# The third tile's modulation product in split operands, in a four-stage gated kernel on one core

## The chip, the cores and the metric

One NeuronCore of a Trainium2 chip runs the whole program. The metric is the device time of one execution in microseconds (us), as the median of several runs. TensorE is PE in the profile, VectorE is DVE, ScalarE is ACT, GpSimd is POOL and SyncE is SP; SPq and ACTq are DMA issues from these engines.

## The reference, cut to what matters

Four residual stages work on x of 4 sequences x 1024 tokens x 512 channels: an MLP with a selected expert, a selected linear layer, a recurrent gated block, and another selected linear layer. The change is in the third, of which these lines matter (`x` is the stage's input):

```python
ctx = causal_ema(x, tau_ctx)
wg = sigmoid(concat([x, ctx]) @ Wg.T + bg);  gated = x * wg
h1 = gelu(x @ Wn1.T + bn1)                     # 128 channels per token
mod = 0.5 + sigmoid(h1 @ Wn2.T + bn2)          # 4 channels per token
traces = [causal_ema(gated * mod[d], tau_raws[d]) for d in range(4)]
temporal = sum_d traces[d] * blend_w[d]
gate = sigmoid(temporal @ Wtemp.T + btemp)
soma = gelu(x @ Wsoma.T + bsoma)
out = layernorm((soma * gate) @ Wout.T) * gamma + beta;  x = x + out
```

## The kernel before, in words

Channels lie on the 128 partitions and tokens along the free axis; a tile is 512 tokens of one sequence, so there are eight tiles, 0 to 7. Matrix products with 128x128 weights are made from split operands: `split_product` issues three matmuls, high weight by high input (L1434), high weight by low input (L1435), low weight by high input (L1436). The high part is a copy by ACT into the type fp32r, the low part is what DVE leaves after subtracting it (`low_part`, L1869).

The order of work on each engine is written out by hand. The engines run their own lists and meet at semaphores. The first two residual stages fill about the first 700 us. Then the recurrent block and the last layer are pipelined by tile: round r of the loops (`for r in range(1, NT)` on PE, `for r in range(2, NT)` on ACT and DVE) takes the gate sums of tile r, the temporal and output products of tile r-1, and the last layer of tile r-2.

The modulation layer of tile i goes as follows. `n1(i)` on PE sums x @ Wn1 into a PSUM bank (L1579 is its last matmul). `h1_of(i)` on ACT makes h1 by GELU (L1058). `mo(i)` on PE multiplies by the 4 columns of Wn2. For tiles 0 to 2 this is one ordinary float32 `matmul` (L1592, two records each in the trace), placed for tile 2 after the first chunk of `gate(2, 0)`, that is after 6 of its 24 matmuls. For tiles 3 to 7 it is a `split_product`, after the second chunk (12 matmuls), and it needs `h1_hi_of(i)` on ACT (L1064) and `h1_low(i)` on DVE (L1869, h_lo). `mod_of(i)` on ACT (L1068) takes the hyperbolic tangent, ACT adds 2 (L1074), writes the four rows to DRAM (L1077) and reads them back on all partitions into mod_t (L1083). The first use of mod_t for a tile is the DVE line `drive` (L2095).

The other chain in the place of the change belongs to tile 1, chunk 3. On DVE `traces_a` to `traces_d` make, from gated, four drives (L2095), four scans (L2108) and three additions (L2123) into temporal. `temporal_hi(1, 3)` on ACT rounds it (L1104), `temporal_low(1, 0)` and `temporal_low(1, 2)` on DVE make the low parts of chunks 0-1 and 2-3 (L1869, temporal_lo). `te(1, 0)` on PE, the first product after `gate(2, 0)`, waits for the first of these low parts, and the next three `te` follow it.

The low part of Wn2 (`wn2_hl`, shown as wn_hl in the trace) is made once, ahead of `temporal_low(1, 0)`.

Of the kernel before, what the change touches and what calls it, by code (L numbers as in the profile page):

```python
# [15 lines left out]
TAUS = 4  # L16
# [25 lines left out]
def build(nc, x, tok16, tok8, small, fc1_w, fc2_w, exp_w, exp_b, l1_w, l1_b, wg, wn1, wsoma, wtemp, wout,  # L42
# [15 lines left out]
    with ctx:  # L58
# [3 lines left out]
        def place(name, kib, shape, dt=F32):  # L62
            return nc.alloc_sbuf_tensor_at(name, [P] + shape, dt, offset=base + int(kib * KIB))
# [7 lines left out]
        def sem(name):  # L71
            return ctx.enter_context(nc.semaphore(name))
# [73 lines left out]
        wn2_hl = place("wn2_hl", 127, [2, P], F32R)  # L146
# [97 lines left out]
        s_wn2 = sem("s_wn2")  # L244
# [201 lines left out]
        def n1_bank(i):  # L446
            return bank[5 if i > 1 else 7]
# [37 lines left out]


        def mo_split_no(i):
            return max(0, i - 2)

        def ss_split_no(i):  # L490
            return min(i, LAST - 1 - 1)
# [10 lines left out]
        def rows_stored(i):  # L502
            return (s_mst, 16 * i) if i else (s_mst_first, 16)
# [416 lines left out]
        def _(eng):  # L920
            on = Once(eng)
# [130 lines left out]
            def h1_of(i):  # L1052
                on.wait_ge(s_pe["N1"], i + 1)
                if i:
                    on.wait_ge(*rows_stored(i - 1))
                if i > 2:
                    on.wait_ge(s_out[1], 16 * HALVES * (i - 2))
                eng.activation(h1[:, :], n1_bank(i)[:, :], ACT.Gelu, bias=bn1_sb[:, 0:1]).then_inc(s_h1, 1)  # L1058


            def h1_hi_of(i):
                on.wait_ge(s_h1, i + 1)
                on.wait_ge(s_pe["SS"], i - 1)
                eng.activation(h1_hi[:, :], h1[:, :], ACT.Copy).then_inc(s_h1hi, 1)  # L1064

            def mod_of(i):
                on.wait_ge(s_pe["MO"], i + 1)
                eng.activation(mod_row[0:TAUS, :], mo_bank(i)[0:TAUS, :], ACT.Tanh, bias=bn2_sb[0:TAUS, 0:1],  # L1068
                               scale=0.5).then_inc(s_mod, 1)


            def modulation_out(i):
                on.wait_ge(s_mod, i + 1)
                eng.activation(mod_row[0:TAUS, :], mod_row[0:TAUS, :], ACT.Identity, bias=two_sb[0:TAUS, 0:1]  # L1074
                               ).then_inc(s_mod2, 1)
                on.wait_ge(s_mod2, i + 1)
                eng.dma_start(mod_dram[i], mod_row[0:TAUS, :]).then_inc(s_mst, 16)  # L1077
# [18 lines left out]
            def temporal_hi(i, m):  # L1096
                on.wait_ge(s_add, SH * (KC * i + m + 1))
                if i:
                    on.wait_ge(s_pe["OU"], KC * i)
                    if m == KC - 1:  # L1100
                        on.wait_ge(s_pe["SS"], min(i, LAST - 1))
                else:
                    on.wait_ge(s_fc2, UNITS)
                eng.activation(ts_hi[:, m, :], temporal[:, m, :], ACT.Copy).then_inc(s_temphi, 1)  # L1104

            def te_tanh(i, m):
                on.wait_ge(s_pe["TE"], KC * i + m + 1)
                ps = te_bank(m)
                eng.activation(ps[:, :], ps[:, :], ACT.Tanh, bias=btemp_sb[:, m:m + 1], scale=0.5
                               ).then_inc(s_gate, 1)  # L1110
# [244 lines left out]
            soma_of(1, 3)  # L1355

            for r in range(2, NT):
                if r == 2:
                    h1_of(r)
                    temporal_hi(r - 1, 3)  # L1360
                else:
                    temporal_hi(r - 1, 3)
                    h1_of(r)
                    h1_hi_of(r)
                mod_of(r)
                modulation_out(r)
                modulation_back(r)
                wg_tanh(r, 0)
                te_tanh(r - 1, 0)
                for m in range(KC):  # L1370
                    x3_hi_of(r - 2, m)
                for m in range(1, KC):
                    te_tanh(r - 1, m)
                for m in range(KC):
                    spikes_hi(r - 1, m)
                wg_tanh(r, 1)
                y_of(r - 2, 0)
                y_of(r - 2, 1)
                if r < LAST:
                    y_of(r - 2, 2)  # L1380
                    y_of(r - 2, 3)
                wg_tanh(r, 2)
                o_of(r - 1, 0)
                o_of(r - 1, 1)
                wg_tanh(r, 3)
                o_of(r - 1, 2)
                o_of(r - 1, 3)
                if r <= LAST - 1:
                    sumsq_hi(r - 1)
                soma_of(r, 0)  # L1390
                soma_of(r, 1)
                for m in range(SH):
                    temporal_hi(r, m)
                if r < LAST:
                    rows_std(r - 1)
                soma_of(r, 2)
                soma_of(r, 3)
# [31 lines left out]
        def _(eng):  # L1429
            on = Once(eng)  # L1430
# [149 lines left out]
                mm.then_inc(s_pe["N1"], 1)  # L1580

            def mo(i):
                if i > 2:

                    on.wait_ge(s_wn2, 3)
                    on.wait_ge(s_h1hi, mo_split_no(i))
                    on.wait_ge(s_h1lo, mo_split_no(i))
                    split_product(mo_bank(i)[:, :], wn2_hl[:, 0, :], wn2_hl[:, 1, :], h1_hi[:, :], h1_lo[:, :],
                                  True, True).then_inc(s_pe["MO"], 1)
                    return  # L1590
                on.wait_ge(s_h1, i + 1)
                eng.matmul(mo_bank(i)[0:TAUS, :], wn2_sb, h1[:, :], start=True, stop=True  # L1592
                           ).then_inc(s_pe["MO"], 1)
# [3 lines left out]
            def gate(i, m):  # L1597
                if m == 0:
                    if i > 1:
                        on.wait_ge(s_soma, KC * (i - 1) + 1)  # L1600
                    elif i:
                        on.wait_ge(s_soma, 1)
                    else:
                        on.wait_ge(s_mod, 1)
                elif m == 1:
                    if i > 1:
                        on.wait_ge(s_mod, i + 1)
                    elif i:
                        on.wait_ge(s_soma, 2)
                    else:  # L1610
                        on.wait_ge(s_x1, KC * LAST)
                elif m == 2:
                    if i >= 2:
                        on.wait_ge(s_z, KC * (i - 1))
                    else:
                        on.wait_ge(s_gated, KC if i else 1)
                else:
                    if i >= 2:
                        on.wait_ge(s_y, KC * (i - 2) + (3 if i < LAST else 1))
                    else:  # L1620
                        on.wait_ge(s_gated, 3 if i else 2)
                        if i:
                            on.wait_ge(s_mod, 2)
                on.wait_ge(s_wg[m], 16)
                for c in range(KC):
                    x2 = slot(i, c)
                    for k, before in ((2 * c, 0), (2 * c + 1, 1)):
                        at = LEAD - before
                        mm = split_product(wg_bank(i, m)[:, :], wg_hl[m][:, k, 0, :], wg_hl[m][:, k, 1, :],
                                           x2[:, 0, at:at + TOK],  # L1630
                                           x2[:, 1, at:at + TOK], c == 0 and not before,
                                           c == KC - 1 and before == 1)
                    if m == 0 and c == (1 if i > 2 else 0) and i > 1:
                        mo(i)
                mm.then_inc(s_pe["WG"], 1)

# [228 lines left out]
        def _(eng):  # L1865
            on = Once(eng)

            def low_part(lo, raw, hi):
                return eng.tensor_tensor(lo, raw, hi.bitcast(F32), ALU.subtract)  # L1869
# [261 lines left out]
            def traces_b(i, c):  # L2131
                trace_of(i, c, 0)
                trace_of(i, c, 1)
                drive_of(i, c, 2)
                add_of(i, c, 1)

            def traces_c(i, c):
                trace_of(i, c, 2)
                drive_of(i, c, 3)
                add_of(i, c, 2)  # L2140
# [10 lines left out]
            def h1_low(i):  # L2151
                on.wait_ge(s_h1hi, mo_split_no(i))
                low_part(h1_lo[:, :], h1[:, :], h1_hi[:, :]).then_inc(s_h1lo, 1)
# [260 lines left out]
            traces_d(1, 2)  # L2414
            traces_a(1, 3)
            traces_b(1, 3)
            traces_c(1, 3)
            traces_d(1, 3)
            on.wait_ge(s_wn2, 2)
            low_part(wn2_hl[:, 1, 0:TAUS], wn2_sb, wn2_hl[:, 0, 0:TAUS]).then_inc(s_wn2, 1)  # L2420
            temporal_low(1, 0)
            temporal_low(1, 2)
            for r in range(2, NT):
# [135 lines left out]
```

## Time and profile before

| | |
|---|---|
| median of 3 runs | 1328.03 us (1327.83 to 1331.12) |
| the profiled execution's own time | 1327.52 us |
| its span, first to last instruction | 1325.8 us |
| PE busy | 1309.0 us (99%) |
| DVE busy | 1060.6 us (80%) |
| ACT busy | 667.6 us (50%) |
| mean granted TensorE clock | 1.000 |

The span leaves 1.72 us of the profiled execution's time around it. A busy share is an average over stages. A matmul's record is 0.39 us long, but matmuls overlap in the pipeline, and one starts every 0.23 us when nothing holds them; so distances between starts are the durations to count with on PE. DVE records overlap in the same way by some 0.07 us.

### The profile page before, as it was taken

Reading aid. Unit: us, or ns where it says so; the run is one execution under the profiler, and the core shown is the slowest. Engines: PE = TensorE matmul, PEld = TensorE weight load, DVE = VectorE, ACT = ScalarE, POOL = GpSimd, SP = SyncE. Lnnn points to the kernel's source line nnn. Section 1 sums busy time; section 2 is a strip of 40 time slices with the busy share of each in tenths; the row PEclk is TensorE's granted clock in tenths of the full one; section 3 lists DMA queues with packets and bytes.
Section 4 is the critical chain, followed back from the end, with each engine's and each line's share of the span. In section 5 each row is a group of like instructions: output and inputs, shape, how many; then the busy total and the mean of one; then the engine's idle time right before and its main releaser. Section 6 shows DMA issues by size and latency. Waiting matters only on the chain.

```text
span 1325.8 us, 16413 instructions
## 1 busy us (share of the span) xinstructions
PE 1309.0 (99%) x5725; PEld 1071.8 (81%) x5725; DVE 1060.6 (80%) x1643; ACT 667.6 (50%) x1237; POOL 102.2 (8%) x135
## 2 busy tenths in 40 slices
PE   8899999999999999999999999999999999999998
PEld 7788788888887887788887887878888888888877
DVE  7877786776787767777645798999999899998985
ACT  6476465755465665456653323434435352525254
POOL 0010010030010000100000100013000210031000
PEclk9999999999999999999999999999999999999999
DMA  8257463765445665536676676512233123212101
GB/s 285 97 167 245 161 163 118 228 169 192 141 139 190 233 215 179 155 113 206 229 236 196 176 228 181 183 50 79 82 127 96 64 96 127 96 65 96 48 16 64
DMA packets 102122, 196.57 MB, mean 148 GB/s; under 512 B 9704, under 2 KB 28136, under 8 KB 98968
## 3 DMA queue, kind: packets, MB, share of 16 engines
q1 hardware_dynamic: 84896, 155.51, 36.9%
q10 hardware_dynamic: 11288, 24.18, 5.9%
q0 software_dynamic: 5856, 15.83, 3.8%
q8 instruction: 46, 0.75, 0.3%
q14 instruction: 36, 0.29, 0.1%
HBM read 125.65 MB, written 69.83 MB: 147 GB/s over the span
## 4 chain that ended last, share of the span: by engine, by line
PE 81%; DVE 12%; issue 2%; ACT 2%; DMA 1%; SPq 1%; DVEq 0%; ACTq 0%
PE bank L1434 27%; PE bank L1435 27%; PE bank L1436 27%; DVE drive L2108 2%; DVE drive L2095 1%; DVE w_hl L1869 1%; DVE h_hl L1869 1%; DVE temporal L2123 1%; DMA hb_in<-hb_dram 1%; DVE temporal L2108 1%; DMA w_raw<-in_exp_w 1%; DVE t_lo L1869 1%; DVE x_raw L2023 1%; DVE x_hl L1869 1%; DVE bank L2071 0%
## 5 line engine op out<-in xcount | busy, mean ns | idle before, releaser
L1434 PE MATMUL bank<-h_hl,w_hl 128*128 128x512 f32 x512 | 199.9, 390 | 4.4 <-DVE w_hl L1869 3.6
L1436 PE MATMUL bank<-h_hl,w_hl 128*128 128x512 f32 x512 | 199.3, 389 | 0.0
L1435 PE MATMUL bank<-h_hl,w_hl 128*128 128x512 f32 x512 | 199.2, 389 | 0.0
L1434 PE MATMUL bank<-t_hi,sp_hl 128*128 128x512 f32 x448 | 175.4, 392 | 6.6 <-DVE hb_out L1963 2.3
L1435 PE MATMUL bank<-t_lo,sp_hl 128*128 128x512 f32 x448 | 174.4, 389 | 0.0
L1436 PE MATMUL bank<-t_hi,sp_hl 128*128 128x512 f32 x448 | 174.3, 389 | 0.0
L1434 PEld LDWEIGHTS bank<-h_hl,w_hl 128*128 128x128 f32 x512 | 96.1, 188 | 27.1 <-DVE h_hl L1869 6.6
L1436 PEld LDWEIGHTS bank<-h_hl,w_hl 128*128 128x128 f32 x512 | 96.1, 188 | 20.1
L1435 PEld LDWEIGHTS bank<-h_hl,w_hl 128*128 128x128 f32 x512 | 96.1, 188 | 19.7
L1434 PEld LDWEIGHTS bank<-t_hi,sp_hl 128*128 128x128 f32 x448 | 84.1, 188 | 28.2 <-ACT p_sb L969 3.5
L1434 PE MATMUL bank<-x_slot,wg_hl 128*128 128x512 f32 x256 | 100.6, 393 | 0.0
L1435 PE MATMUL bank<-x_slot,wg_hl 128*128 128x512 f32 x256 | 99.8, 390 | 0.0
L1436 PE MATMUL bank<-x_slot,wg_hl 128*128 128x512 f32 x256 | 99.4, 388 | 0.0
L1436 PEld LDWEIGHTS bank<-t_hi,sp_hl 128*128 128x128 f32 x448 | 84.1, 188 | 17.5
L1435 PEld LDWEIGHTS bank<-t_lo,sp_hl 128*128 128x128 f32 x448 | 84.1, 188 | 17.1
L2095 DVE SCALAR_TENSOR_TENSOR drive<-gated,small_sb,mod_t 128x512 f32<-128x512 f32 x128 | 92.0, 739 | 1.9 <-DVE gated L2079 0.2
L1869 DVE TENSOR_TENSOR w_hl<-w_raw,w_hl 128x512 fp32r<-128x512 f32 x128 | 86.5, 684 | 8.3 <-ACT w_hl L961 7.1
L961 ACT ACTIVATE w_hl<-w_raw 128x512 fp32r<-128x512 f32 x128 | 78.4, 620 | 8.4 <-PE bank L1436 6.3
L1028 ACT ACTIVATE h_hl<-hb_in 128x512 fp32r<-128x512 f32 x64 | 40.1, 627 | 81.3 <-DMA hb_in<-hb_dram 43.6
L1869 DVE TENSOR_TENSOR h_hl<-hb_in,h_hl 128x512 fp32r<-128x512 f32 x64 | 43.9, 685 | 36.9 <-ACT h_hl L1028 36.9
L945 ACT ACTIVATE sp_hl<-s_raw_sb 128x256 fp32r<-128x256 f32 x128 | 50.7, 410 | 35.2 <-PE bank L1436 28.8
L2123 DVE TENSOR_TENSOR temporal<-drive,temporal 128x512 f32<-128x512 f32 x96 | 65.8, 686 | 1.0
(226 smaller groups left out, 2849.9 us busy)
## 6 DMA issues: line engine op xcount, KB each, us to landing
fc_raw<-in_fc_w SPq DMA_DIRECT2D x32, 512.0 KB, 4.4
hb_dram<-hb_out SPq DMA_DIRECT2D x64, 256.0 KB, 3.1
hb_in<-hb_dram ACTq DMA_DIRECT2D x64, 256.0 KB, 3.0
x2hl_dram<-x_hl POOLq DMA_DIRECT2D x28, 512.0 KB, 7.1
x_slot<-x2hl_dram SPq DMA_DIRECT2D x26, 513.0 KB, 5.2
stage<-in_l_w SPq DMA_DIRECT2D x32, 256.0 KB, 3.5
x_raw<-in_x SPq DMA_DIRECT2D x8, 1024.0 KB, 7.0
x_dram<-x_raw SPq DMA_DIRECT2D x8, 1024.0 KB, 7.9
```

The costliest lines, as they stand in the source:

```text
L945: eng.activation(sp_hl[n % RING][:, 0, :, :], product_source(n), ACT.Copy).then_inc(s_shi, 1)
L961: eng.activation(w2_hl[v % 3][:, 0, :, :], w2_raw[:, j, :, :], ACT.Copy).then_inc(s_w2hi, 1)
L1028: eng.activation(h_hl[v % 4][:, 0, :], hb_in[v % 4][:, :], ACT.Copy).then_inc(s_hhi, 1)
L1434: eng.matmul(ps, w_hi, x_hi, start=first, stop=False, skip_group_check=resumed)
L1435: eng.matmul(ps, w_hi, x_lo, start=False, stop=False, skip_group_check=resumed)
L1436: return eng.matmul(ps, w_lo, x_hi, start=False, stop=final, skip_group_check=resumed)
L1869: return eng.tensor_tensor(lo, raw, hi.bitcast(F32), ALU.subtract)
L2023: eng.scalar_tensor_tensor(xr, acc_of_tile(t)[m][:, :], bias, xr, ALU.add, ALU.add).then_inc(s_x1, 1)
L2095: eng.scalar_tensor_tensor(drive[d % 2][:, :], gated[:, :], blend_sb[:, TAUS * c + d:TAUS * c + d + 1], mod_t[:, d, :], ALU.mult, ALU.mult ...
L2108: eng.tensor_tensor_scan(traced, alpha[:, 1 + d:2 + d].to_broadcast([P, TOK]), drive[d % 2][:, :], start, ALU.mult, ALU.add).then_inc(s_tr ...
L2123: eng.tensor_tensor(temporal[:, c, :], drive[d % 2][:, :], temporal[:, c, :], ALU.add).then_inc(s_add, 1)
```

## The change

Tile 2's modulation product becomes a `split_product`, as those of tiles 3 to 7 are, and moves from after the first chunk to after the second chunk of `gate(2, 0)`. On ACT, h1's rounding for tile 2 is added behind `h1_of(2)` and ahead of `temporal_hi(1, 3)`. On DVE, the low part of Wn2 and the low part of h1 are made between `traces_b(1, 3)` and `traces_c(1, 3)`. The counts that the waits use are raised by one (`mo_split_no`).

```diff
         def mo_split_no(i):
-            return max(0, i - 2)
+            return max(0, i - 1)
...
             for r in range(2, NT):
+                if r > 2:
+                    temporal_hi(r - 1, 3)
+                h1_of(r)
+                h1_hi_of(r)
                 if r == 2:
-                    h1_of(r)
                     temporal_hi(r - 1, 3)
-                else:
-                    temporal_hi(r - 1, 3)
-                    h1_of(r)
-                    h1_hi_of(r)
                 mod_of(r)
...
             def mo(i):
-                if i > 2:
+                if i > 1:
...
-                    if m == 0 and c == (1 if i > 2 else 0) and i > 1:
+                    if m == 0 and c == 1 and i > 1:
                         mo(i)
...
             traces_b(1, 3)
+            on.wait_ge(s_wn2, 2)
+            low_part(wn2_hl[:, 1, 0:TAUS], wn2_sb, wn2_hl[:, 0, 0:TAUS]).then_inc(s_wn2, 1)
+            h1_low(2)
             traces_c(1, 3)
             traces_d(1, 3)
-            on.wait_ge(s_wn2, 2)
-            low_part(wn2_hl[:, 1, 0:TAUS], wn2_sb, wn2_hl[:, 0, 0:TAUS]).then_inc(s_wn2, 1)
             temporal_low(1, 0)
             temporal_low(1, 2)
```

## Rows read from the trace of the kernel before

**Rows 1.** Page, section 1: busy us and share, number of instructions.
```profile
PE 1309.0 (99%) x5725; PEld 1071.8 (81%) x5725; DVE 1060.6 (80%) x1643; ACT 667.6 (50%) x1237; POOL 102.2 (8%) x135
```
**Rows 2.** Waits of PE from 868.4 us to the end.
```profile
PE bank L1434 <- DVE h_lo L1869: 0.4, 1, 0.4
PE bank L1434 <- DVE temporal_lo L1869: 0.2, 1, 0.2
PE bank L1434 <- DVE spikes_lo L1869: 0.2, 1, 0.2
```
**Rows 3.** Timeline of PE: start us, us, line, operation, [idle before <- releaser].
```profile
861.01 0.39 PE L1434 MATMUL bank<-x_slot,wg_hl 128*128 128x512 f32 x1
...
862.15 0.39 PE L1436 MATMUL bank<-x_slot,wg_hl 128*128 128x512 f32 x1
862.86 1.02 PE L1592 MATMUL bank<-h,small_sb 128*4 128x512 f32 x2 [0.33 <-ACT h L1058]
863.81 0.50 PE L1434 MATMUL bank<-x_slot,wg_hl 128*128 128x512 f32 x1
864.15 0.40 PE L1435 MATMUL bank<-x_slot,wg_hl 128*128 128x512 f32 x1
...
867.82 0.39 PE L1436 MATMUL bank<-x_slot,wg_hl 128*128 128x512 f32 x1
868.37 0.47 PE L1434 MATMUL bank<-ts_hi,wtemp_hl 128*128 128x512 f32 x1 [0.16 <-DVE temporal_lo L1869]
```
**Rows 4.** Timeline of DVE, tile 1's last chunk and what follows.
```profile
861.97 0.68 DVE L2123 TENSOR_TENSOR temporal<-drive,temporal 128x512 f32<-128x512 f32 x1
862.57 1.28 DVE L2108 TENSOR_TENSOR_SCAN drive<-alpha,trace_last,drive 128x512 f32<-128x512 f32 x1
...
866.93 0.15 DVE L1869 TENSOR_TENSOR wn_hl<-small_sb,wn_hl 128x4 fp32r<-128x4 f32 x1
867.00 2.35 DVE L1869 TENSOR_TENSOR temporal_lo<-temporal,ts_hi 128x1024 fp32r<-128x1024 f32 x2
869.27 3.34 DVE L2179 RECIPROCAL rstd<-rstd 128x512 f32<-128x512 f32 x1
...
879.79 1.41 DVE L2095 SCALAR_TENSOR_TENSOR drive<-gated,small_sb,mod_t 128x512 f32<-128x512 f32 x2
```
**Rows 5.** Timeline of ACT, from tile 1's soma on.
```profile
860.97 1.26 ACT L1126 ACTIVATE soma<-bank,small_sb 128x512 f32<-128x512 f32 x2
862.12 0.69 ACT L1058 ACTIVATE h<-bank,small_sb 128x512 f32<-128x512 f32 x1
867.04 0.63 ACT L1104 ACTIVATE ts_hi<-temporal 128x512 fp32r<-128x512 f32 x1 [4.24 <-DVE temporal L2123]
867.58 0.66 ACT L1068 ACTIVATE mod_row<-bank,small_sb 4x512 f32<-4x512 f32 x1
...
870.44 0.81 ACTq L1083 DMA_DIRECT2D mod_t<-mod_dram  x2
```
**Rows 6.** Timeline of tile 4's h1 on ACT and DVE.
```profile
1001.94 0.69 ACT L1058 ACTIVATE h<-bank,small_sb 128x512 f32<-128x512 f32 x1 [0.81 <-PE bank L1579]
...
1003.33 0.69 DVE L1869 TENSOR_TENSOR h_lo<-h,h_hi 128x512 fp32r<-128x512 f32 x1 [0.60 <-ACT h_hi L1064]
1003.94 3.35 DVE L2179 RECIPROCAL rstd<-rstd 128x512 f32<-128x512 f32 x1
```
**Rows 7.** Timeline around tile 3's split modulation product, DVE's low part first.
```profile
934.17 0.68 DVE L1869 TENSOR_TENSOR h_lo<-h,h_hi 128x512 fp32r<-128x512 f32 x1
...
935.00 0.47 PE L1434 MATMUL bank<-h_hi,wn_hl 128*128 128x512 f32 x1 [0.39 <-DVE h_lo L1869]
...
935.77 0.39 PE L1434 MATMUL bank<-x_slot,wg_hl 128*128 128x512 f32 x1
```
**Rows 8.** Windows: busy PE, PEld, DVE, ACT, POOL; clock; DMA share; GB/s.
```profile
868.00:935.00 67.00, 66.45 (x291) 54.38 (x291) 66.17 (x79) 28.25 (x48) 16.85 (x16) 1.00 0.23 79
935.00:1289.00 354.00, 354.00 (x1554) 291.45 (x1555) 333.19 (x386) 145.75 (x233) 31.31 (x32) 1.00 0.24 80
44.00:50.00 6.00, 6.00 (x27) 4.95 (x27) 5.05 (x11) 2.88 (x8) 0.00 (x0) 1.00 0.16 59
```
**Rows 9.** Tile mod_t, 860 to 890 us: its loads' time to landing.
```profile
DMA to landing us min/median/max: 3.9/4.9/5.9
```
**Rows 10.** Timeline of PE early in the first stage, a long wait.
```profile
43.79 0.50 PE L1434 MATMUL bank<-t_hi,sp_hl 128*128 128x512 f32 x1 [2.28 <-DVE hb_out L1963]
```

## The prediction, made before the changed kernel ran

> **What bounds the kernel now.** I read the busy shares first. PE is busy for 1309.0 us of a span of 1325.8 us, DVE for 80% [rows 1]. That says that PE is the engine to watch, and not yet what the place of the change costs, since shares are averages. So I read PE's waits next, over the part of the span in which and after which the change lies. From 868.4 us to the end there are three waits, 0.8 us together [rows 2], and in the 354 us from 935 to 1289 PE is busy for all 354.00 [rows 8]. Whatever moves PE's work at 868 us therefore moves the end by as much; there is no gap behind it in which a delay could vanish.
>
> What sets the start of PE's work at 868 us? In PE's timeline the last matmul of gate(2, 0) starts at 867.82. The step is 0.23 us, so te(1, 0) could start at 868.05. It starts at 868.37, and the releaser named is DVE's temporal_lo [rows 3]. DVE's timeline shows it working without a gap up to that instruction at 867.00, and behind it [rows 4]; it is busy for 66.17 of the 67 us that follow [rows 8]. At this one place the bound is DVE, by 0.32 us, and DVE is full for a round thereafter. The change puts work, and a wait, on DVE just there.
>
> **PE's own part.** Without a modulation product the seventh matmul of gate(2, 0) would start one step after 862.15, at 862.38, and the eighth at 862.61. The eighth starts at 864.15 [rows 3]. The float32 product costs PE 864.15 - 862.61 = 1.54 us, 0.33 of it a wait for h1. The split one is three steps: from 935.00 to 935.77 is 0.77 us with the restart after a wait [rows 7]. So the instructions themselves give back 1.54 - 0.77 = 0.77 us, if nothing else happens.
>
> When can the split product start? Its 12 leading matmuls end their turn at 861.01 + 12 x 0.228 = 863.74. Its last input is h1_lo. Tile 4 shows the chain GELU, rounding, low part with an idle ACT and a waiting DVE: from the start of h at 1001.94 to the start of h_lo at 1003.33 is 1.39 us [rows 6]. h of tile 2 starts at 862.12, behind the soma activations [rows 5], and nothing of the change is ahead of it on ACT. So h_lo starts at 862.12 + 1.39 = 863.51. Tile 3 shows 935.00 - 934.17 = 0.83 us from the start of h_lo to the first matmul on it [rows 7]: 864.34. PE waits 0.60 us, longer than it did for h1 itself. The gate goes on 0.77 later, at 865.11, and its other 12 matmuls end their turn at 865.11 + 12 x 0.228 = 867.85. That is 0.20 us earlier than the 868.05 of before. Of PE's 0.77 us, 0.57 go into the longer way to the start, and the 0.20 left reach te(1, 0) ahead of its input.
>
> **DVE's part.** Before, the third scan of chunk 3 (traces_c) starts at 862.57 [rows 4]. Now Wn2's low part stands in front of it, which moves its 0.07 us step (866.93 to 867.00) from later to earlier and adds nothing to the sum; then h_lo, which can't start before 863.51. The instruction behind an h_lo starts 1003.94 - 1003.33 = 0.61 us after it [rows 6]: 864.12. So traces_c starts 864.12 - 862.57 = 1.55 us later, and temporal_lo 1.55 - 0.07 = 1.48 us later, at 868.48. Of the 1.48 us, 0.61 is the new instruction and 0.87 is DVE standing still behind a semaphore with traces_c, traces_d and temporal_low ready behind it: DVE reaches h_lo at 862.57 + 0.07 = 862.64 and finds it ready at 863.51.
>
> te(1, 0) waits for the first temporal_lo and starts at 868.37 + 1.48 = 869.85. PE ends the gate at 867.85 and stands for 2.0 us, where it stood 0.32. The second temporal_lo starts some 1.15 us after the first and is needed six matmuls (1.37 us) into te(1, 0) at about its end, in the same distance as before, so it adds nothing.
>
> What bounds DVE's delay? Below, an h_lo that finds its input ready costs 0.61 - 0.07 = 0.54 us, as tile 3's does, which follows its predecessor at once [rows 7]; above, the 1.48 us and perhaps 0.3 us more if ACT's h, its soma and the semaphores lie a little later than in tile 4. I take 1.48, since the distances of tile 4 are of the same three instructions on the same operands.
>
> The Trainium skill speaks against the way I count here. "VectorE: DVE Perf Modes", section "Rules for kernel authors", says of chained DVE operations: "Minimize op *count*, not sems". By it one added operation is all that is paid, and the sum would be +0.54 us. The rule is about semaphores that are already satisfied; the row of tile 4 shows DVE idle 0.60 us for one that is not [rows 6], so I keep the larger number and give the smaller one a chance below.
>
> **ACT's part and the modulation's way back.** ACT gains one rounding (0.63 us, in a gap of 4.24 us between h and the rounding of temporal [rows 5]); that gap hides it, and uncovered it would cost 0.6 us. temporal_hi(1, 3) still comes when the last addition does: 867.04 + 1.48 = 868.52, and it isn't late for the second temporal_lo. mod_of(2) stands behind it and goes from 867.58 to 869.06. Its two issues on ACT's queue (store and reload) go with it, the reload from 870.44 to 871.92. With the longest landing of 5.9 us [rows 9] after the second of the two, which is issued 0.4 us on, mod_t is there near 878.2. Its first use moves from 879.79 [rows 4] to 881.27. The distance stays 3 us. SP's and POOL's lists don't hold anything of the change.
>
> **Later rounds.** From 868 to 935 us DVE has no gap [rows 8] and everything in its list starts 1.48 us later; PE's work does too. The wait of 0.39 us for tile 3's h_lo [rows 7] stays as it is, since both sides have moved alike. If DVE alone could catch up there, that wait would shrink and the sum would be 1.48 - 0.39 = +1.09. I see nothing that would let it. After that PE runs alone and keeps its delay.
>
> **Sum.** +1.48 us on the profiled execution: 1327.52 + 1.48 = 1329.00. The profiled execution lies 0.51 us under the median of the runs shown, 1328.03, so for the median I say 1328.03 + 1.48 = 1329.5. The case's own range is +1.1 to +2.1 us.
>
> **Rivals.**
> 1. *Only the instruction is paid* (+0.54, 1328.6). h_lo's input is ready when DVE comes to it. It would need h to start 0.87 us earlier, and ACT is full with tile 1's soma up to then [rows 5]. Chance 0.07.
> 2. *Not slower* (-0.2, 1327.8). In the runs that count, te(1, 0) is not held by DVE at all; PE's 0.20 us is then a gain, and DVE's delay falls into slack. It decides at one place: with the delay counted, DVE would have to run 869.85 - 867.85 = 2.0 us earlier against PE than it does in this trace; in its favour is that 2.0 us is little against the length of a round, and that DVE has real slack from tile 4 on (idle before h_lo, 0.60 us [rows 6]). Against it: both engines are tied to each other by the products of tile 1 just before, and the distance should be the same in every run. Chance 0.12.
> 3. *TensorE loses its clock in the 2.0 us stand.* Four te products are 48 matmuls, 10.9 us by 0.228. At the lower of the two levels, 1.2 GHz, each start would be 0.23 us later, and if it lasted over all four the sum is 1.48 + 10.9: 1340.4. Against it stands the wait of 2.28 us at 43.79 [rows 10], behind which the granted clock is 1.00, that is 2.4 GHz, and 27 matmuls start in 6 us [rows 8]. Chance 0.03.
> 4. *A further shift of unknown kind*, more than +2.1: mod_t's 3 us used up, or a DMA of another queue that meets the reload. Chance 0.06.
>
> Beside rival 3: "TensorE: Matmul & The Clock Gate", Part 1, of the Trainium skill says that the default state is throttled and that activity releases it; by that page a long enough stand gives the clock back, and a change that lengthens a stand is suspect. The row at 43.79 has a stand of this size without it.
>
> **Numbers.** The forecast has 0.72. A difference under 0.3%, 4 us, is what a measurement of this kernel can't tell from no change. Everything but rival 3 and a part of rival 4 lies within it: same 0.93; slower 0.05 (0.03 from rival 3, 0.02 from rival 4); faster 0.02 for what I haven't seen. The range for 8 in 10 takes the forecast's own range and rivals 1 and 2, with the spread of a median of few runs (the three shown have two within 0.2 us and one 3 us above): 1327.6 to 1331.5.
>
> **What would show it.** In the changed kernel's trace: h_lo of tile 2 near 863.5 with about 0.9 us idle before it, and traces_c near 864.1; the split product near 864.3 with a wait of about 0.6 us; te(1, 0) near 869.85 with a wait on temporal_lo of near 1.8 us, against 0.16 in its record before; mod_of near 869.1; then the same distances as before, to the end, and three PE waits after 868 us. The prediction is wrong if te(1, 0) starts before 869.4 or after 870.5, if a wait of PE appears or goes in a later round, or if the granted clock falls behind the stand.

## The result, and the profile after

The changed kernel takes 1330.59 us (median of 20 runs, 1328.25 to 1333.57) against 1328.16 us before (20 runs, 1326.04 to 1331.17). The ratio is 1.0015 with a 95% interval of 1.0009 to 1.0022, that is +2.0 us with +1.2 to +2.9 (the two medians lie 2.43 us apart, the two means 1.99). The forecast was +1.48 us, inside the interval, and 1329.5 us for the median, with 1327.6 to 1331.5 as its range. The difference is under the 0.3% that was called no change.

The page of the changed kernel, section 1 (against [rows 1]): one weight load and matmul more, one DVE and one ACT instruction more.
```profile
PE 1311.1 (99%) x5726; PEld 1074.1 (81%) x5726; DVE 1061.0 (80%) x1644; ACT 668.0 (50%) x1238; POOL 102.2 (8%) x135
```
Lines behind L488 have moved up by one: L1433 to L1435 are the three matmuls of `split_product`, L1868 is `low_part`. PE's waits from 850 us on in the changed kernel (engine, line, releaser: total us, times, longest):
```profile
PE bank L1433 <- DVE temporal_lo L1868: 1.8, 1, 1.8
PE bank L1433 <- DVE h_lo L1868: 0.8, 2, 0.4
PE bank L1433 <- DVE spikes_lo L1868: 0.2, 1, 0.2
```
Against [rows 2], the wait on temporal_lo has grown from 0.2 to 1.8 us, and h_lo is waited for twice: once for tile 3, as before, and once for tile 2. PE has no new kind of wait later on, in this trace.

DVE in the changed kernel (start us, us, line, operation, [idle before <- releaser]):
```profile
863.48 0.69 DVE L2122 TENSOR_TENSOR temporal<-drive,temporal 128x512 f32<-128x512 f32 x1
864.08 0.15 DVE L1868 TENSOR_TENSOR wn_hl<-small_sb,wn_hl 128x4 fp32r<-128x4 f32 x1
865.02 0.69 DVE L1868 TENSOR_TENSOR h_lo<-h,h_hi 128x512 fp32r<-128x512 f32 x1 [0.78 <-ACT h_hi L1064]
865.63 1.28 DVE L2107 TENSOR_TENSOR_SCAN drive<-alpha,trace_last,drive 128x512 f32<-128x512 f32 x1
...
869.99 2.35 DVE L1868 TENSOR_TENSOR temporal_lo<-temporal,ts_hi 128x1024 fp32r<-128x1024 f32 x2
```
PE in the changed kernel:
```profile
865.04 0.39 PE L1435 MATMUL bank<-x_slot,wg_hl 128*128 128x512 f32 x1
865.86 0.47 PE L1433 MATMUL bank<-h_hi,wn_hl 128*128 128x512 f32 x1 [0.43 <-DVE h_lo L1868]
...
866.63 0.40 PE L1433 MATMUL bank<-x_slot,wg_hl 128*128 128x512 f32 x1
...
869.15 0.39 PE L1435 MATMUL bank<-x_slot,wg_hl 128*128 128x512 f32 x1
871.35 0.47 PE L1433 MATMUL bank<-ts_hi,wtemp_hl 128*128 128x512 f32 x1 [1.81 <-DVE temporal_lo L1868]
```
These times can't be laid beside those of before as they stand, since everything ahead of the change is later in this execution. The first matmul of n1(2) is a common mark ahead of the change; it starts at 858.29 before and at 859.81 here, 1.52 us later. The kernels don't differ up to it. The reader should count from that mark, and all experiments below do:

```
                      before   changed   difference
h1 on ACT starts        3.83     3.83       0.00
h_lo of tile 2           -       5.21
gate(2, 0), last mm     9.53     9.34      -0.19
temporal_lo starts      8.71    10.18      +1.47
te(1, 0) starts        10.08    11.54      +1.46
tile 3's split product 76.71    78.18      +1.47
tile 7's split product 354.39   355.88     +1.49
end of the span        467.51   468.99     +1.48
```

So the two profiled spans, 1325.8 and 1328.8 us, differ by 3.0 us, of which 1.48 lie behind the mark and belong to the change, and 1.52 ahead of it and don't. Where those come from, the windows of the changed kernel show (busy PE, PEld, DVE, ACT, POOL; granted clock; DMA share; GB/s):
```profile
40.00:44.00 4.00, 1.72 (x7) 1.11 (x7) 3.97 (x11) 2.12 (x5) 0.00 (x0) 1.00 0.60 179
44.00:46.00 2.00, 2.00 (x7) 1.58 (x8) 1.88 (x4) 2.00 (x6) 0.00 (x0) 0.68 0.37 137
46.00:48.00 2.00, 2.00 (x6) 1.62 (x5) 1.53 (x5) 0.68 (x3) 0.00 (x0) 0.50 0.09 33
48.00:50.00 2.00, 2.00 (x10) 1.55 (x9) 0.06 (x1) 0.00 (x0) 0.00 (x0) 0.96 0.00 0
866.00:868.00 2.00, 2.00 (x9) 1.62 (x10) 2.00 (x3) 0.00 (x0) 0.00 (x0) 1.00 0.00 0
872.00:874.00 2.00, 2.00 (x11) 1.64 (x10) 2.00 (x2) 0.06 (x1) 0.00 (x0) 1.00 0.01 4
```
TensorE fell to 0.50, its lower level of 1.2 GHz, behind the long stand in the first stage, and stayed at 2.4 GHz behind the one that the change makes. The 18 matmul starts from 43.91 us, behind the first stand, take 5.83 us here, to 49.74; the same 18 take 4.22 us in the trace of before, from 43.79 to 48.01. That is 1.61 us, about the whole of the 1.52.
```profile
43.91 0.50 PE L1433 MATMUL bank<-t_hi,sp_hl 128*128 128x512 f32 x1 [2.28 <-DVE hb_out L1962]
...
46.39 0.63 PE L1434 MATMUL bank<-t_lo,sp_hl 128*128 128x512 f32 x1
46.81 0.63 PE L1435 MATMUL bank<-t_hi,sp_hl 128*128 128x512 f32 x1
```
This stand in the first stage is as long as before's [rows 10], behind which the clock stayed up in the execution of before.

### The profile page after: what moved, and what is told of

It is laid out like the page before. It is cut to its first block, busy times and chain, and to the rows that moved or that the text cites. A ratio compares the mean times of both kernels' runs of the same rounds, so it can differ in the third digit from the quotient of the medians.

```text
span 1328.8 us, 16418 instructions
## 1 busy us (share of the span) xinstructions
PE 1311.1 (99%) x5726; PEld 1074.1 (81%) x5726; DVE 1061.0 (80%) x1644; ACT 668.0 (50%) x1238; POOL 102.2 (8%) x135
## 3 DMA queue, kind: packets, MB, share of 16 engines
q1 hardware_dynamic: 84896, 155.51, 36.9%
## 4 chain that ended last, share of the span: by engine, by line
PE 81%; DVE 12%; ACT 2%; issue 2%; DMA 1%; SPq 1%; DVEq 0%; ACTq 0%
PE bank L1433 27%; PE bank L1434 27%; PE bank L1435 27%; DVE drive L2107 2%; DVE w_hl L1868 1%; DVE h_hl L1868 1%; DVE drive L2094 1%; DVE temporal L2122 1%; DMA hb_in<-hb_dram 1%; DVE temporal L2107 1%; DVE t_lo L1868 1%; DMA w_raw<-in_exp_w 1%; DVE x_raw L2022 1%; DVE x_hl L1868 1%; DVE bank L2070 0%
## 5 line engine op out<-in xcount | busy, mean ns | idle before, releaser
L1433 PE MATMUL bank<-h_hl,w_hl 128*128 128x512 f32 x512 | 199.9, 391 | 3.5 <-DVE w_hl L1868 3.2
L1435 PE MATMUL bank<-h_hl,w_hl 128*128 128x512 f32 x512 | 199.3, 389 | 0.0
L1433 PE MATMUL bank<-t_hi,sp_hl 128*128 128x512 f32 x448 | 176.3, 394 | 6.6 <-DVE hb_out L1962 2.3
L1435 PE MATMUL bank<-t_hi,sp_hl 128*128 128x512 f32 x448 | 174.8, 390 | 0.0
L1433 PEld LDWEIGHTS bank<-h_hl,w_hl 128*128 128x128 f32 x512 | 96.1, 188 | 26.6 <-DVE h_hl L1868 5.0
L1435 PEld LDWEIGHTS bank<-h_hl,w_hl 128*128 128x128 f32 x512 | 96.1, 188 | 20.0
L1433 PEld LDWEIGHTS bank<-t_hi,sp_hl 128*128 128x128 f32 x448 | 84.5, 189 | 28.4 <-ACT p_sb L969 3.5
L1433 PE MATMUL bank<-x_slot,wg_hl 128*128 128x512 f32 x256 | 100.5, 393 | 0.0
L1435 PE MATMUL bank<-x_slot,wg_hl 128*128 128x512 f32 x256 | 99.4, 388 | 0.0
L1435 PEld LDWEIGHTS bank<-t_hi,sp_hl 128*128 128x128 f32 x448 | 84.6, 189 | 17.6
L1868 DVE TENSOR_TENSOR w_hl<-w_raw,w_hl 128x512 fp32r<-128x512 f32 x128 | 86.5, 684 | 8.3 <-ACT w_hl L961 7.0
L1868 DVE TENSOR_TENSOR h_hl<-hb_in,h_hl 128x512 fp32r<-128x512 f32 x64 | 43.8, 685 | 37.3 <-ACT h_hl L1028 37.3
```

The lines of the kernel that those rows point to most:

```text
L1433: eng.matmul(ps, w_hi, x_hi, start=first, stop=False, skip_group_check=resumed)
L1435: return eng.matmul(ps, w_lo, x_hi, start=False, stop=final, skip_group_check=resumed)
```

## The experiments

Each was compared with the kernel before on the same chip. All positions are us behind the first matmul of n1(2), read from each kernel's own trace; "product 3" is the first matmul of tile 3's split product. The runs of the kernel before lie 5 to 8 us apart within a group, so a ratio's interval is about 0.1% to either side. The positions carry the verdicts. They come from one profiled execution of each kernel, and they repeat within 0.05 us where nothing was changed, up to tile 5's product. Behind that, a wait for a transfer comes in some executions and not in others (see c_before).

```
              te(1, 0)  product 3   ratio to before (95%)
before          10.08     76.71
c_before        10.07     76.72     0.9999 (0.9990 to 1.0009)
changed         11.54     78.18     1.0015 (1.0009 to 1.0022)
e_fill          11.46     78.20     1.0011 (1.0002 to 1.0020)
e_dve_only      11.55     78.19     1.0008 (0.9999 to 1.0017)
e_pe_only       10.08     76.72     1.0000 (0.9991 to 1.0009)
e_ready         10.69     77.35     1.0005 (0.9996 to 1.0014)
e_early          9.37     77.51     1.0008 (0.9999 to 1.0017)
e_both           9.37     76.58     0.9991 (0.9981 to 1.0000)
e_both_split     8.88     77.25     1.0004 (0.9995 to 1.0013)
e_cover          9.38     75.97     0.9987 (0.9976 to 0.9999)
e_cover_split    8.88     76.65     1.0003 (0.9990 to 1.0016)
e_third         10.09     76.13     0.9993 (0.9981 to 1.0005)
```

**c_before, the kernel before against itself.** No edit.

> The kernel before, unchanged, timed against itself, to see how much single executions scatter and what the mean granted TensorE clock of each is. Theory (the added time is DVE's 1.5 us ahead of te(1, 0), and the scatter is the same in both kernels): ratio 1.000, and clocks from 0.996 to 1.000 here too, since the stand of 2.28 us early in the first stage is in this kernel as well. Rival (the longer stand of the changed kernel at te(1, 0) costs the clock in some executions, and makes up the difference between 1.5 and the measured 2.0 us): the mean clock here is higher than the changed kernel's 0.9984, by 0.0004 or more.

The ratio is 0.9999, and the positions repeat within 0.01 us up to tile 3 and within 0.03 us up to tile 5. Then tile 6's product comes at 285.62, 0.63 us later than in the other execution of the same kernel (284.99). PE's weight loads (PEld) show why: they stand for a reload of x_slot.
```profile
1144.28 0.19 PEld L1576 LDWEIGHTS bank<-x_slot,wn_hl 128*128 128x128 f32 x1 [0.55 <-DMA x_slot<-x2hl_dram]
...
1144.93 0.19 PEld L1579 LDWEIGHTS bank<-x_slot,wn_hl 128*128 128x128 f32 x1 [0.35 <-DMA x_slot<-x2hl_dram]
```
The reload was issued at the same place in both (279.73 and 279.75 us behind the mark), so it was the transfer that took longer. The same wait costs 0.35 to 0.60 us in six of the thirteen traces: c_before, e_pe_only, e_ready, e_early, e_both and e_cover_split. The kernel before, the changed one, e_cover and e_third, whose later positions are compared here, don't have it. Of the 4.8 us between the spans of c_before (1330.6) and before (1325.8), 4.10 lie ahead of the mark, where c_before's clock is at 0.50 from 10 to 14 us, and 0.60 are this wait.

The mean clock of c_before's own 11 runs is 0.9989, which is 0.0005 above the changed kernel's 0.9984, as the rival asked for. Over all 95 runs of before that came with the three groups of experiments it is 0.9988. But these 95 runs are in three groups with means of 0.9986, 0.9988 and 0.9991, which lie as far apart. By itself this doesn't decide; e_fill does more.

**e_fill, TensorE's stand filled.**
```diff
+                if r == 2:
+                    on.wait_ge(s_std, 1)
+                    for _ in range(8):
+                        eng.matmul(te_bank(1)[:, :], wg_hl[0][:, 0, 0, :], x2_slot[x2_at(2, 0)][:, 0, LEAD:],
+                                   start=True, stop=True)
                 for m in range(KC):
                     te(r - 1, m)
```


> The changed kernel with 8 more matmuls (1.8 us) between gate(2, 0) and te(1, 0), whose results are overwritten; they fill TensorE's stand there and leave DVE alone. Theory (DVE's chain sets te(1, 0), and the stand itself costs nothing): te(1, 0) stays 11.5 us behind the first matmul of n1(2), as in the changed kernel, the filled TensorE costs at most 0.1 us, ratio to before 1.001 to 1.0015. Rival (the stand gives the clock away in some executions): the mean clock rises over the changed kernel's 0.9984 by about 0.0004 and the time falls by some 0.5 us, ratio 1.0007 to 1.0011.

```profile
869.23 0.39 PE L1435 MATMUL bank<-x_slot,wg_hl 128*128 128x512 f32 x1
869.46 1.99 PE L1829 MATMUL bank<-x_slot,wg_hl 128*128 128x512 f32 x8
871.36 0.50 PE L1433 MATMUL bank<-ts_hi,wtemp_hl 128*128 128x512 f32 x1
```
PE now works up to te(1, 0), and te(1, 0) comes at 11.46, 0.08 us earlier than in the changed kernel, of which nothing is left at tile 3's product (78.20). The mean clock of its 11 runs is 0.9984, the same as the changed kernel's: it didn't rise as the rival said. So the stand itself costs neither time nor clock that these runs can tell, though a difference of 0.0003, such as lies between two groups of before, would not be seen; it is room that nothing uses.

**e_dve_only, the loss without the split product.** On ACT, h1_of(2), h1_hi_of(2) and then temporal_hi(1, 3), as in the change, and mod_of(2) waits for the low part, too; on DVE:
```diff
             traces_b(1, 3)
+            on.wait_ge(s_wn2, 2)
+            low_part(wn2_hl[:, 1, 0:TAUS], wn2_sb, wn2_hl[:, 0, 0:TAUS]).then_inc(s_wn2, 1)
+            on.wait_ge(s_h1hi, 1)
+            low_part(h1_hi[:, :], h1[:, :], h1_hi[:, :]).then_inc(s_h1lo, 1)
             traces_c(1, 3)
             traces_d(1, 3)
-            on.wait_ge(s_wn2, 2)
-            low_part(wn2_hl[:, 1, 0:TAUS], wn2_sb, wn2_hl[:, 0, 0:TAUS]).then_inc(s_wn2, 1)
```


> The kernel before, with its float32 product for tile 2 in its old place, plus the change's work on ACT and DVE alone: h1's rounding ahead of temporal_hi(1, 3), and one low part of it between traces_b(1, 3) and traces_c(1, 3), which nothing of the product uses. Theory: the whole loss is there without the split product, te(1, 0) starts 10.08 + 1.48 = 11.5 to 11.6 us behind the first matmul of n1(2), ratio 1.001 to 1.0015. Rival (the split product on TensorE, its 128-column weights and its later place, makes a part of the loss): te(1, 0) at less than 11.2, ratio 1.0000 to 1.0007.

DVE, then PE, of e_dve_only (L1872 is `low_part`, L1595 the float32 product):
```profile
865.47 0.69 DVE L1872 TENSOR_TENSOR h_hi<-h,h_hi 128x512 fp32r<-128x512 f32 x1 [0.78 <-ACT h_hi L1064]
866.08 1.28 DVE L2111 TENSOR_TENSOR_SCAN drive<-alpha,trace_last,drive 128x512 f32<-128x512 f32 x1
```
```profile
864.83 1.02 PE L1595 MATMUL bank<-h,small_sb 128*4 128x512 f32 x2 [0.33 <-ACT h L1058]
871.81 0.47 PE L1437 MATMUL bank<-ts_hi,wtemp_hl 128*128 128x512 f32 x1 [1.64 <-DVE temporal_lo L1872]
```
TensorE runs its old list here, with its old wait of 0.33 us, and te(1, 0) is at 11.55 all the same. The whole delay comes from DVE's list. The rival, that the split product makes a part of the loss, is out.

**e_pe_only, the split product without DVE's work.** The low part of h1 is left out, and with it the wait for it.
```diff
-                    on.wait_ge(s_h1lo, mo_split_no(i))
-                    split_product(mo_bank(i)[:, :], wn2_hl[:, 0, :], wn2_hl[:, 1, :], h1_hi[:, :], h1_lo[:, :],
+                    on.wait_ge(s_h1lo, i - 2)
+                    split_product(mo_bank(i)[:, :], wn2_hl[:, 0, :], wn2_hl[:, 1, :], h1_hi[:, :],
+                                  h1_lo[:, :] if i > 2 else h1_hi[:, :],
...
-            h1_low(2)
```


> The changed kernel without the low part of tile 2's h1 on DVE: the third factor of the split product is the high part once more, so the result lacks the low part's correction. Theory: DVE is as in the kernel before; the split product starts at 863.74 by before's clock, without a wait, gate(2, 0) ends 0.8 us earlier than before (near 867.2), and none of it reaches the end, as te(1, 0) waits for temporal_lo and starts 10.08 us behind the first matmul of n1(2), as before; ratio 1.0000. Rival (TensorE bounds the place and its saving of 0.8 us is kept): te(1, 0) at 9.3, ratio 0.9994.

```profile
862.94 0.39 PE L1435 MATMUL bank<-x_slot,wg_hl 128*128 128x512 f32 x1
863.17 0.40 PE L1433 MATMUL bank<-h_hi,wn_hl 128*128 128x512 f32 x1
863.40 0.39 PE L1434 MATMUL bank<-h_hi,wn_hl 128*128 128x512 f32 x1
863.63 0.39 PE L1435 MATMUL bank<-h_hi,wn_hl 128*128 128x512 f32 x1
...
866.37 0.39 PE L1435 MATMUL bank<-x_slot,wg_hl 128*128 128x512 f32 x1
867.79 0.47 PE L1433 MATMUL bank<-ts_hi,wtemp_hl 128*128 128x512 f32 x1 [1.03 <-DVE temporal_lo L1869]
```
Without a wait the split product takes 3 x 0.23 us, and the last matmul of gate(2, 0) starts 8.66 us behind the mark instead of 9.53: PE has gained 0.87 us. Then it waits 1.03 us for temporal_lo, and te(1, 0) is at 10.08, as before. The saving on the busiest engine is worth nothing here, since DVE sets the next thing it does.

**e_ready, the low part where its input is ready.**
```diff
-            h1_low(2)
             traces_c(1, 3)
+            h1_low(2)
             traces_d(1, 3)
...
-                    if m == 0 and c == 1 and i > 1:
+                    if m == 0 and c == (1 if i > 2 else 2) and i > 1:
```


> The changed kernel with h1's low part one step later on DVE, between traces_c(1, 3) and traces_d(1, 3), where its input is ready, and the split product after the third chunk (18 matmuls) of gate(2, 0). Theory (of DVE's 1.47 us, 0.61 is the instruction and 0.87 the standing still ahead of it): te(1, 0) starts 10.08 + 0.54 = 10.62 us behind the first matmul of n1(2), tile 3's product at 77.25, ratio to before 1.0004. Rival (the place doesn't matter, what costs is that the split product waits for three engines in a row): te(1, 0) stays at 11.5.

DVE in e_ready has no idle time ahead of h_lo:
```profile
864.98 0.69 DVE L2122 TENSOR_TENSOR temporal<-drive,temporal 128x512 f32<-128x512 f32 x1
865.59 0.69 DVE L1868 TENSOR_TENSOR h_lo<-h,h_hi 128x512 fp32r<-128x512 f32 x1
866.19 1.28 DVE L2107 TENSOR_TENSOR_SCAN drive<-alpha,trace_last,drive 128x512 f32<-128x512 f32 x1
```
te(1, 0) comes at 10.69, +0.61 against before: the instruction alone. The other 0.85 us of the changed kernel's 1.46 were DVE's standing still. The rival, that the place doesn't matter, is out. The expectation of 10.62 was 0.07 too low; it took the moved step of Wn2's low part off once too often.

**e_early, te(1, 0) freed.** In the kernel before, temporal_low(1, 0) goes ahead of traces_c(1, 3), te(1, 0) and te(1, 1) run as a pair, and the float32 product goes after the second chunk:
```diff
+            def te_pair(i):
...
+                for half in range(2):
+                    on.wait_ge(s_templo, KC * i + 2 * half + 2)
+                    for m in range(2):
+                        for c in (2 * half, 2 * half + 1):
...
             traces_b(1, 3)
+            temporal_low(1, 0)
             traces_c(1, 3)
             traces_d(1, 3)
...
-            temporal_low(1, 0)
             temporal_low(1, 2)
```


> The kernel before with three places moved and no arithmetic changed: temporal_low(1, 0) between traces_b(1, 3) and traces_c(1, 3), te(1, 0) and te(1, 1) as a pair that takes chunks 0 and 1 of both first, and tile 2's float32 product after the second chunk of gate(2, 0). Theory (DVE bounds two places in a row, te(1, 0) and tile 3's split product): te(1, 0) starts 0.7 us earlier, 9.4 us behind the first matmul of n1(2), but tile 3's split product stays at 76.7, with PE's wait for h_lo grown from 0.4 to 1.1 us; ratio 1.0000. Rival (te(1, 0) is the only such place): tile 3's product at 76.3 or less, ratio 0.9995 to 0.9997.

te(1, 0) comes 0.71 us earlier, as both theories had it, but tile 3's product comes at 77.51, 0.8 us *later* than before, which neither had. PE's wait for h_lo there grew from 0.39 to 0.82 us. The step that was missed shows in DVE's timeline of e_both, which has the same order at this place (L1888 is `low_part`), and e_early's has the same idle 0.69 us:
```profile
860.67 1.22 DVE L1888 TENSOR_TENSOR temporal_lo<-temporal,ts_hi 128x1024 fp32r<-128x1024 f32 x1
...
866.17 0.15 DVE L1888 TENSOR_TENSOR wn_hl<-small_sb,wn_hl 128x4 fp32r<-128x4 f32 x1
867.02 1.23 DVE L1888 TENSOR_TENSOR temporal_lo<-temporal,ts_hi 128x1024 fp32r<-128x1024 f32 x1 [0.69 <-ACT ts_hi L1104]
```
The first temporal_low, in its old place, covered ACT's rounding of chunk 3 (0.63 us). Taken away, it leaves DVE idle 0.69 us ahead of the second.

**e_both, tile 3's place too.**
```diff
+                elif r == 3:
+                    h1_of(r)
+                    h1_hi_of(r)
+                    temporal_hi(r - 1, 3)
...
-                if r > 2:
+                if r > 3:
                     h1_low(r)
...
                 temporal_low(r, 0)
+                if r == 2:
+                    h1_low(3)
                 temporal_low(r, 2)
```


> As e_early, and at tile 3 ACT makes h1 and its rounding ahead of temporal_hi(2, 3) and DVE makes h1's low part between temporal_low(2, 0) and temporal_low(2, 2). Theory: both places are freed, tile 3's split product comes 75.6 us behind the first matmul of n1(2), 1.1 us earlier than before, and the end with it, ratio 0.9992. Rival (DVE's list as a whole bounds this round, so that the delay comes back at a later wait of the round): tile 4's product not earlier than before, ratio 1.0000.

Tile 3's product is at 76.58 and not at 75.6. PE no longer waits there, but it has lost its lead on the way, first at 36.9 us behind the mark, where a weight load waits for ACT, then where tile 1's sum of squares is taken:
```profile
893.33 0.19 PEld L1438 LDWEIGHTS bank<-x_hi,l3w_hl 128*128 128x128 f32 x1 [0.47 <-ACT y_sb L1185]
...
921.05 0.47 PE L1723 MATMUL bank<-ts_hi,ones 128*128 128x512 f32 x1 [0.17 <-ACT ts_hi L1160]
921.69 0.50 PE L1725 MATMUL bank<-sumsq_lo,ones 128*128 128x512 f32 x1 [0.16 <-DVE sumsq_lo L1888]
```
Counted by the distances between starts, the first place costs 0.31 us and the second 0.84; in the kernel before there is no loss at either. DVE was 0.8 us late in this round (the second temporal_low at 10.63 behind the mark, 9.86 before) from the uncovered rounding, and PE was 0.7 us early, so that hand-overs which had slack before now hold PE; e_cover below takes DVE's part away. The rival's mechanism, a delay that comes back at a later wait of the round, was right in kind, though not its number (tile 4's product is at 146.00, 0.19 us earlier than before).

**e_both_split.** The same with the split product for tile 2: h1_low(2) behind the early temporal_low(1, 0), the product after the third chunk.

> As e_both, with tile 2's product split as in the changed kernel: h1's low part for tile 2 behind the early temporal_low(1, 0), where its input is ready, and the product after the third chunk. Theory (the split product costs DVE 0.54 us even without a wait, and DVE sets tile 3's product): tile 3's product at 76.1, 0.5 us behind e_both and 2.1 us ahead of the changed kernel, ratio to before 0.9996. Rival (TensorE's saving of 0.5 us against the float32 product comes out once the waits are gone): tile 3's product at 75.1 to 75.6, at or ahead of e_both.

77.25, where 76.1 was expected, and 0.67 us behind e_both: both are late against their forecasts by the uncovered rounding, and the distance between them is near that of one h_lo (0.61). The rival, that PE's saving comes out, is out. The ratio of 1.0004 can't tell it from before.

**e_cover, the rounding covered again.** e_both with chunk 2's low part by itself:
```diff
-            temporal_low(1, 2)
+            temporal_low(1, 2, 1)
+            temporal_low(1, 3, 1)
```


> As e_both, with the low parts of tile 1's chunks 2 and 3 made one by one, chunk 2 first. In e_both DVE stood 0.77 us for ACT's rounding of chunk 3, which the low part of chunks 0 and 1 had covered; chunk 2's low part (0.6 us) should cover it. Theory (that uncovered rounding delayed DVE, and DVE's delay came back to PE at the row sums and at tile 3's product): the first low part of chunk 2 at 9.9 us behind the first matmul of n1(2) instead of 10.6, tile 3's product at 75.9 instead of 76.6, ratio to before 0.9994. Rival (PE lost its lead through the paired order of te, which stays here): tile 3's product stays at 76.6.

```profile
870.74 1.40 DVE L1888 TENSOR_TENSOR temporal_lo<-temporal,ts_hi 128x512 fp32r<-128x512 f32 x2
```
The first of the two starts 9.85 us behind the mark, against 10.63 in e_both, and tile 3's product is at 75.97, 0.74 us ahead of before. The rival, that the paired order made e_both's loss, would have left it at 76.6 and is out. The ratio is 0.9987 (0.9976 to 0.9999): this version is ahead of the kernel before, by some 1.7 us by the ratio and by 0.8 us by positions (its end is 466.71 behind the mark, before's 467.51). The measured ratio alone would allow anything from 0.1 to 3.2 us. PE still loses 0.64 us at tile 1's sum of squares.

**e_cover_split.** e_cover with the split product for tile 2.

> As e_cover, with the split product for tile 2 as in e_both_split. Theory (the split's one DVE instruction, 0.61 us, is paid in full wherever DVE bounds, and PE's smaller product gives nothing back): tile 3's product 0.6 us later than in e_cover, at 76.5, ratio to before 0.9999. Rival (with the waits gone PE's saving of 0.5 us counts): tile 3's product at or ahead of e_cover's.

76.65, 0.68 us behind e_cover. PE waits at three hand-overs of that round where e_cover has one, and at a fourth (L1723) only at 420 us behind the mark, near the end, where e_ready waits too and before doesn't; why is open, and product 3 lies ahead of it:
```profile
PE bank L1723 <- DVE sumsq L2185: 0.3, 1, 0.3
PE bank L1433 <- DVE temporal_lo L1883: 0.2, 1, 0.2
PE bank L1718 <- ACT ts_hi L1160: 0.2, 1, 0.2
PE bank L1720 <- DVE sumsq_lo L1883: 0.2, 1, 0.2
```
te(1, 0) is 0.50 us earlier than in e_cover, which is PE's saving by the smaller product; tile 3's product is 0.68 us later, which is DVE's one instruction. In this order, too, the split of tile 2 loses.

**e_third.** The kernel before with the tile 3 part of e_both alone.

> The kernel before with only the tile 3 part of e_both: h1 and its rounding ahead of temporal_hi(2, 3) on ACT, h1's low part between the two temporal_low on DVE. Theory (each of the two places holds PE by its own): te(1, 0) at 10.08 us behind the first matmul of n1(2) as before, PE's wait of 0.4 us for h_lo gone, tile 3's product at 76.15 instead of 76.71, ratio 0.9996. Rival (the wait moves to te(2, 0), whose second low part is now 0.6 us later): the distance from tile 3's to tile 4's product grows by as much as was won.

te(1, 0) at 10.09 and tile 3's product at 76.13, 0.58 us earlier than before. From there to tile 4's product it is 69.40 us, against 69.48 before, and to tile 7's 277.60 us, against 277.68, so no wait has grown in its place, and the rival is out. This part of e_cover stands by itself, and it is most of e_cover: with te(1, 0) 0.70 us earlier on top, e_cover's tile 3 product is only 0.16 us ahead of e_third's, since PE loses most of that lead again at tile 1's sum of squares, where e_third loses nothing.

## Why the prediction was right

*DVE sets te(1, 0), and PE's saving doesn't reach the end.* Shown from both sides: e_pe_only has the saving and not the delay and is at 10.08; e_dve_only has the delay and not the saving and is at 11.55.

*DVE's delay of 1.48 us.* Measured 1.47 to temporal_lo and 1.46 to te(1, 0). h_lo was forecast 5.22 behind the mark and came at 5.21; its predecessor left DVE idle for 0.78 us by the record, 0.87 by starts.

*Its division into 0.61 and 0.87 us.* e_ready measures the first as 0.61 and leaves 0.85. The lower bound was mis-sized: I gave 0.54, taking off a step that had only moved. It should have been 0.61. The rule of the Trainium skill that counts operations and not semaphores ("VectorE: DVE Perf Modes", "Rules for kernel authors") holds in e_ready, where the semaphore is satisfied, and falls short by 0.85 us in the changed kernel, where it isn't.

*PE's split product at 864.34, gate(2, 0) 0.20 us shorter.* Measured by before's clock: 865.86 - 1.52 = 864.34, and the gate 0.19 us shorter.

*A shift that stays to the end.* Measured +1.47 at tile 3, +1.49 at tile 7, +1.48 at the end. The wait of 0.39 us at tile 3 stayed (0.41). The prediction said that DVE has no gap from 868 to 935 us, where its rows have 66.17 of 67 us busy; the rest are pieces of at most 0.10 us between instructions, so the reading holds. That nothing later could take up a delay holds for these two traces. In six others tile 6 waits for a transfer, 0.35 to 0.60 us; whether such a wait would take up a part of the 1.48 us is open, as none of the three traces with the whole delay has it.

*The modulation's way back.* mod_of(2) was forecast 1.48 later; it starts at 870.64 against 867.58, less 1.52 is +1.54. Nothing waited for mod_t.

*TensorE keeps its clock behind the 2.0 us stand.* It did in the trace, and e_fill, without the stand, has the same mean clock. The mean clock of single runs can't exclude a rare fall (c_before). The prediction's argument for it was weak, though: it took one quiet execution behind the stand of 2.28 us as evidence, and the changed kernel's execution shows the clock falling behind that very stand. It also had the price too high: a start at the lower level comes 0.20 us later (0.43 instead of 0.23) and not 0.23, which makes 9.6 us of the 10.9 for 48 matmuls. The Trainium skill ("TensorE: Matmul & The Clock Gate", Part 1) says that an idle TensorE falls back to its throttled state. That bears on this kernel at a place that both versions share: behind the stand of 2.28 us the trace of the changed kernel shows it (0.50), the trace of before doesn't (1.00).

*The other rivals.* Rival 2 had te(1, 0) not held by DVE in the runs that count. It is at 10.08, 10.07 and 10.08 in the three traces without DVE's added work (before, c_before, e_pe_only) and at 11.54, 11.46 and 11.55 in the three with it (changed, e_fill, e_dve_only). Rival 1 needed h_lo's input ready, and DVE stood 0.78 us for it. Of rival 4 no run shows anything.

*The size.* The measured +2.0 us (+1.2 to +2.9) holds 1.48. What the rest of 0.5 us is stays open: the interval is wide enough for it to be nothing, and e_dve_only, which has the same delay, measured 1.0008 (0.9999 to 1.0017). Pooling the two wouldn't settle it, as they ran in different groups.

## What to carry to other kernels

A saving on the busiest engine counts only where that engine isn't waiting next; look at the releaser of its next wait before counting it, and charge the edit to the engine that the releaser names. Two costs stand in front of an instruction that is inserted into a full, in-order list: its own step, and the time until its input is ready, and here the second was the larger one (0.87 of 1.48 us); one place further down the list made it zero. When an instruction is moved forward, ask what it covered where it stood: here 1.1 us of low part hid a rounding on another engine, and moving it without a substitute put tile 3's product 0.8 us later, although te(1, 0) had become 0.7 us earlier. And a lead that one engine wins can be lost at the next hand-over: of e_cover's 0.70 us at te(1, 0), 0.16 reached tile 3's product.

## What the runs showed of the hardware

The clock of TensorE behind one and the same wait of 2.28 us differed between executions: it stayed at 2.4 GHz in the profiled execution of before and fell to 1.2 GHz in that of the changed kernel, where the matmuls from 45.11 to 47.67 us start 0.43 us apart instead of 0.23. In nine of the thirteen traces the clock is below 1.00 in some stretch, in eight of them in the first 50 us; these falls lie outside the place of the change. In the 95 single runs of before, those with a mean clock of 1.000 average 1327.75 us (22 runs) and those with 0.997 average 1331.11 us (10 runs). So a part of the scatter goes with the clock, though not all of it: the 46 runs at 0.999 alone spread from 1326.95 to 1334.01. The wait for x_slot at tile 6, 0.35 to 0.60 us in six of thirteen traces, is another part. A position counted from a mark behind the early falls and read ahead of tile 6 resolves 0.05 us where a median resolves about 1.
